# Softmax row sums of groups three to six by a VectorE reduction instead of ScalarE's accumulators

## The reference

```python
attn = jnp.einsum('bhtd,bhsd->bhts', q, k) * scale
attn = jnp.where(causal, -jnp.inf, attn)
attn = jax.nn.softmax(attn, axis=-1)
out = jnp.einsum('bhts,bhsd->bhtd', attn, v)
out = out.transpose(0, 2, 1, 3).reshape(b, t, NH * D)
return out @ Wo
```

## Time and profile before

| | |
|---|---|
| median of three runs | 156.2 us (156.09 to 156.68) |
| the profiled execution | 156.23 us |
| its span, first to last instruction | 154.4 us |
| granted TensorE clock, mean | 1.000 of full speed |
| TensorE matmuls busy | 148.3 us |
| VectorE busy | 118.5 us |
| ScalarE busy | 101.7 us |
| GpSimd busy | 60.0 us |

### The profile page before, as it was taken

One profiled execution on the slowest core, in us unless ns is written; L12 is line 12 of the kernel. 1 busy time (PEld: TensorE's weight loads), 2 busy tenths in 40 slices (PEclk: granted clock), 3 DMA queues, 4 the chain that ended last, 5 costly groups with the idle time before them and its releaser, 6 DMA issues.

```text
span 154.4 us, 3280 instructions
## 1 busy us (share of the span) xinstructions
PE 148.3 (96%) x1089; PEld 138.9 (90%) x1089; DVE 118.5 (77%) x370; ACT 101.7 (66%) x290; POOL 60.0 (39%) x50
## 2 busy tenths in 40 slices
PE   6999999999999999999999999799999999999992
PEld 2778789899998699999989999799999999999991
DVE  0058777898988967577765766999798995999792
ACT  0306997798999779998883496856456564654700
POOL 0004998454486344407326000334534336045100
PEclk9999999999999999999999999999999999999999
DMA  5999910000000299800000000000000000000004
GB/s 150 326 373 375 409 31 0 0 4 4 0 0 0 40 406 427 350 5 8 0 0 4 0 0 0 0 4 2 0 2 4 0 0 2 0 4 0 4 2 157
DMA packets 5891, 11.95 MB, mean 77 GB/s; under 512 B 930, under 2 KB 3698, under 8 KB 5746
## 3 DMA queue, kind: packets, MB, share of 16 engines
q1 hardware_dynamic: 4434, 9.79, 17.4%
q10 hardware_dynamic: 1440, 1.95, 3.6%
HBM read 11.13 MB, written 0.61 MB: 76 GB/s over the span
## 4 chain that ended last, share of the span: by engine, by line
PE 81%; DVE 7%; ACT 6%; DMA 3%; issue 1%; ACTq 1%; DVEq 0%
PE bank L1053 61%; PE bank L1142 5%; PE bank L1170 5%; PE bank L1077 3%; DMA x_sb<-xT 3%; PE bank L1068 2%; PE bank L1158 2%; ACT act L538 1%; ACT act_hi L541 1%; DVE hn L716 1%; ACT L545 1%; DVE stats L694 1%; PE bank L1097 1%; DVE h L839 1%; DVE rrest L809 0%
## 5 line engine op out<-in xcount | busy, mean ns | idle before, releaser
L411 POOL TENSOR_TENSOR exp_lo<-ffn_sb,exp_hi 128x512 fp32r<-128x512 f32 x18 | 24.2, 1351 | 43.4 <-ACT exp_hi L529 40.4
L842 DVE SCALAR_TENSOR_TENSOR h<-bank,gate,h 128x256 f32<-128x256 f32 (+1 forms) x80 | 32.7, 471 | 1.5 <-PE bank L1053 1.3
L1053 PE MATMUL bank<-exp_hi,act_hi 128*128 128x256 f32 (+1 forms) x90 | 25.7, 285 | 0.8 <-DVE h L842 0.8
L1053 PE MATMUL bank<-exp_hi,act_lo 128*128 128x256 f32 (+1 forms) x90 | 25.3, 281 | 0.0
L1053 PE MATMUL bank<-exp_lo,act_hi 128*128 128x256 f32 (+1 forms) x90 | 25.3, 281 | 0.0
L822 DVE TENSOR_TENSOR act_lo<-act,act_hi 128x256 fp32r<-128x256 f32 (+1 forms) x36 | 19.4, 571 | 3.4 <-ACT act_hi L541 3.0
L1053 PE MATMUL bank<-hnT_hi,exp_hi 128*128 128x256 f32 (+1 forms) x72 | 21.6, 300 | 0.0
L529 ACT ACTIVATE exp_hi<-ffn_sb 128x512 fp32r<-128x512 f32 x18 | 11.4, 635 | 15.3 <-PE bank L1053 15.3
L1053 PE MATMUL bank<-hnT_lo,exp_hi 128*128 128x256 f32 (+1 forms) x72 | 21.5, 298 | 0.0
L1053 PE MATMUL bank<-hnT_hi,exp_lo 128*128 128x256 f32 (+1 forms) x72 | 21.5, 298 | 0.0
L396 POOL TENSOR_TENSOR swapped<-swapped,sin_sb 128x512 f32<-128x512 f32 (+1 forms) x12 | 16.4, 1367 | 10.2 <-ACT swapped L496 10.1
(11 more groups left out here) (92 smaller groups left out, 370.7 us busy)
## 6 DMA issues: line engine op xcount, KB each, us to landing
ffn_sb<-w_ffn SPq DMA_DIRECT2D x6, 768.0 KB, 8.3
wqkv_sb<-w_qkv SPq DMA_DIRECT2D x4, 512.0 KB, 8.8
wo_sb<-w_o SPq DMA_DIRECT2D x1, 1024.0 KB, 11.1
x_sb<-xT ACTq DMA_DIRECT2D x2, 384.0 KB, 6.5
out<-h SPq DMA_DIRECT2D x2, 256.0 KB, 2.2
x_sb<-xT ACTq DMA_DIRECT2D x3, 128.0 KB, 4.6
wp_sb<-wpT SPq DMA_DIRECT2D x3, 128.0 KB, 3.7
wp_sb<-wpT ACTq DMA_DIRECT2D x3, 128.0 KB, 4.9
```

Source lines behind the costliest of these rows:

```text
L411: nc.gpsimd.tensor_tensor(exp_lo[:, e % SPLIT_RING, :], ffn_sb[:, e, :], exp_hi[:, e % SPLIT_RING, :].bitcast(F32), ALU.subtract).then_inc ...
L842: last = nc.vector.scalar_tensor_tensor(h[r, i, :], y, gate[r, i, one], h[r, i, :], ALU.mult, ALU.add)
L1053: last = nc.tensor.matmul(ps, a, b, start=(n == 0 and m == 0), stop=(n == len(pairs) - 1 and m == 2 and not more))
```

## The change

For groups 2 to 5, `exps` no longer adds up the rows. `inv_sum` begins with one VectorE `tensor_reduce` over the quad (111 x 4 rows of 111, or 74 x 4 rows of 74), which writes `ssum`, and waits on a new semaphore `sc_sum` before the reciprocal. Groups 0 and 1 stay as they were. With this, all four lists are written anew, from the first layer norm to the last expert; no step is added or dropped in them. The diff, with the stretches of the lists that matter most:

```diff
+SUMMED = 2
...
+        sc_sum = sem("sc_sum")
...
         @block.gpsimd
-            for n in range(0, 9):
+            for n in range(0, 8):
                 sine(n)
             normalise(0, 0)
+            sine(8)
             sine(9)
+            normalise(0, 1)
             sine(10)
-            normalise(0, 1)
             sine(11)
...
             normalise(2, 1)
+            low_parts(0)
             normalise(3, 0)
...
             def exps(g, c):
                 for j in range(QUAD):
                     hd = QUAD * c + j
                     scores_of = probs[0:GN[g], g % 2, hd, 0:GN[g]]
-                    last = nc.scalar.activation(scores_of, scores_of, ACT.Exp, bias=slow[0:GN[g], g, hd:hd + 1], scale=-1.0,
-                                                accum_out=ssum[0:GN[g], g, hd:hd + 1])
+                    less = slow[0:GN[g], g, hd:hd + 1]
+                    if g < SUMMED:
+                        last = nc.scalar.activation(scores_of, scores_of, ACT.Exp, bias=less, scale=-1.0,
+                                                    accum_out=ssum[0:GN[g], g, hd:hd + 1])
+                    else:
+                        last = nc.scalar.activation(scores_of, scores_of, ACT.Exp, bias=less, scale=-1.0)
                 last.then_inc(sc_exp, 1)
...
             def inv_sum(g, c):
                 dve.wait_ge(sc_exp, 2 * g + c + 1)
+                if g >= SUMMED:
+                    nc.vector.tensor_reduce(ssum[0:GN[g], g, QUAD * c:QUAD * c + QUAD], quad(probs, g, c),
+                                            AX_X, ALU.add).then_inc(sc_sum, 1)
+                    dve.wait_ge(sc_sum, 2 * (g - SUMMED) + c + 1)
                 nc.vector.reciprocal(sinv[0:GN[g], g, QUAD * c:QUAD * c + QUAD],
                                      ssum[0:GN[g], g, QUAD * c:QUAD * c + QUAD]).then_inc(sc_inv, 1)
```

More of the change, by code:

```diff
@@ L436, in _ @@
             normalise(5, 1)
-            for n in range(2, 18):
+            for n in range(1, 18):
                 low_parts(n)
@@ L593, in _ @@
             keep_pT(0, 1)
+            exps(1, 1)
             heads_high(0, 0)
@@ L878, in _ @@
             norm_apply(2)
+            norm_apply(3)
             turned_low(0)
             turned_low(1)
-            norm_apply(3)
             norm_stats(4)
@@ L886, in _ @@
             cosine(1)
+            turned_low(3)
             rope_add(0)
@@ L889, in _ @@
             cosine(3)
-            turned_low(3)
             turned_low(4)
-            rope_add(1)
-            rope_add(2)
+            for n in range(1, 4):
+                rope_add(n)
+            cosine(4)
+            cosine(5)
+            rope_add(4)
+            rope_add(5)
             wo_low()
-            cosine(4)
+            cosine(6)
             less_max(0, 0)
[L897 to L902, removed]
             cosine(7)
@@ L905, in _ @@
             rope_add(7)
+            inv_sum(0, 0)
+            less_max(0, 1)
+            less_max(1, 0)
             cosine(8)
-            less_max(1, 0)
             cosine(9)
+            inv_sum(0, 1)
             rope_add(8)
+            rope_add(9)
+            cosine(10)
+            rope_add(10)
             less_max(1, 1)
-            inv_sum(0, 1)
-            cosine(10)
             cosine(11)
-            for n in range(9, 12):
-                rope_add(n)
             inv_sum(1, 0)
+            rope_add(11)
+            less_max(2, 0)
             inv_sum(1, 1)
-            less_max(2, 0)
             heads_low(0, 0)
@@ L928, in _ @@
             less_max(4, 0)
+            less_max(4, 1)
+            heads_low(2, 0)
+            heads_low(2, 1)
             inv_sum(3, 0)
-            less_max(4, 1)
             inv_sum(3, 1)
@@ L977, in _ @@
             add_expert(1, 1)
-            act_low(6)
-            act_low(7)
             add_expert(1, 2)
+            for n in range(6, 9):
+                act_low(n)
             add_expert(2, 0)
@@ L983, in _ @@
             add_expert(2, 2)
-            act_low(8)
-            act_low(9)
             add_expert(3, 0)
             add_expert(3, 1)
-            act_low(10)
-            act_low(11)
+            for n in range(9, 13):
+                act_low(n)
             add_expert(3, 2)
@@ L998, in _ @@
             add_expert(5, 2)
+            for n in range(13, 16):
+                act_low(n)
             add_expert(6, 0)
-            for n in range(15, 18):
-                act_low(n)
             add_expert(6, 1)
             add_expert(6, 2)
+            act_low(16)
             add_expert(7, 0)
+            act_low(17)
             add_expert(7, 1)
@@ L1008, in _ @@
             add_expert(8, 1)
-            for n in range(18, 22):
+            act_low(18)
+            act_low(19)
+            add_expert(8, 2)
+            for n in range(20, 23):
                 act_low(n)
-            add_expert(8, 2)
             add_expert(9, 0)
@@ L1014, in _ @@
             add_expert(9, 2)
+            act_low(23)
             add_expert(10, 0)
-            for n in range(22, 27):
-                act_low(n)
             add_expert(10, 1)
@@ L1330, in _ @@
             down(1, 1)
-            up(8)
             down(1, 2)
             down(2, 0)
-            up(9)
+            for n in range(8, 12):
+                up(n)
             down(2, 1)
@@ L1355, in _ @@
             down(7, 0)
-            for n in range(17, 21):
-                up(n)
+            up(17)
+            up(18)
             down(7, 1)
@@ L1361, in _ @@
             down(8, 1)
+            up(19)
             down(8, 2)
-            up(21)
-            up(22)
+            for n in range(20, 24):
+                up(n)
             down(9, 0)
```

228 lines of the change are left out of this document (111 added, 117 removed).

## The result

The changed kernel takes 157.42 us (median of 5 runs, 157.07 to 157.71), the kernel before 156.6 in the same comparison. The ratio is 1.0056, 95% interval 1.0038 to 1.0074: 0.8 to 0.9 us slower, where I forecast 0.3 us faster, and outside my range (154.7 to 157.1). The profiled execution took 157.07 us with a span of 155.2, 0.8 more than before.

What follows compares the result with a forecast made beforehand. The prediction took TensorE to bound the kernel, busy 148.3 of 154.4 us. A walk through its waits took 0.3 us off the span, to 154.1; with the 1.83 us around it 155.9 us, range 154.7 to 157.1.

Steps and rivals of the forecast that it cites:

- Row sums cost nothing in the new lists: Groups 2 to 5: reductions add 4.2 us to VectorE, hidden between exps and normalise; at the high bound 0.8 us.
- Relief of ScalarE is not relief of the kernel: From 60 to 65 us ScalarE is busy for all 5.00 us, but so is TensorE; nobody waits for ScalarE.
- First layer norm, 0.1: norm_apply(3) ahead of turned_low(0) and (1) delays the first projection 0.55 us, but costs only 0.1 at cosine(0).
- First attention groups: From about 52 us: 0.6 and 0.3 us gained, given back by VectorE; TensorE through at 57.3 as before.
- Third output projection: It ends at 76.6, before 76.0, with turn_probs(4, ...) ahead of it and a short wait for heads_low(3, 1).
- Statistics, inv_std, two keep_pT, ..., 80.4: The fourth output projection waits for keep_turned(6) until 80.4, where before it was 80.57; gain 0.2 us.
- Router: router_exp ends at 94.4; the long TensorE stretch starts at 98.4, before 98.58: earlier 0.2 gain kept, nothing added.
- Experts, no wait: In the long TensorE stretch: the same 411-odd matmuls, and no wait found in the new order.
- The returned waits are not there: Faster rival: without the waits for heads_low(0, ...) and keep_turned(6), 1.2 us less, 154.7 us; chance 0.32.
- VectorE and GpSimd collide: Slower rival: rope_add(11) behind normalise(1, 0) delays scores(2, 1) by 1.0 us: 156.9, with slow sums 157.4; chance 0.14.
- A wait in the expert stage: Slower rival: six down pieces in a row outrun VectorE's sums, 0.5 to 1 us: 156.7 to 157; chance 0.09.
- Nothing moves: Rival: TensorE's work is the same and every gain is given back, 156.2 us; chance 0.12.

Runs made afterwards that it cites:

- the lists alone: New lists, with ScalarE's accumulators kept for all six groups and no reduction on VectorE, against the kernel before: 157.72 us, ratio 1.0080.
- the new tail alone: Old lists up to the last output projection, new lists from there on, accumulators kept, against the kernel before: 156.31 us, ratio 0.9979.

## Why the prediction was wrong

**What held.** The prices: 0.28 us a step for an exponential, reductions of 0.60 and 0.44, 3.0 us less on ScalarE (I took 2.9, of 2.9 to 5.4). *Row sums cost nothing in the new lists*: shown by the lists alone, which are not faster. *Relief of ScalarE is not relief of the kernel*: shown for the old lists without any sums (0.9996); in the new lists it is relief, of some 0.3 to 0.4 us. *First layer norm, 0.1*: 0.12 in the two profiles, but `project(2)` starts anywhere from 23.08 to 24.13 in the fourteen profiles, so this is not resolved.

**The step that failed** is the forecast that the returned waits between 52 and 81 us leave a gain of 0.2 us. They leave a loss of 0.9. By starts of equal work after `project(2)`, 0.2 to 0.3 us of it are there at `scores(3, 0)`, 0.4 come at `project_out(2)` and 0.35 behind `attend(4, 0)`; 0.1 is won back between them.

- *First attention groups, "net: nothing"*: +0.4 (0.26 after `project(2)`). I had VectorE's times right: `heads_low(0, 0)` and `(0, 1)` ended at 56.45 and 56.97, forecast 56.3 and 56.9. But I let TensorE be through 0.4 us after the second, and compared that with an end in the chain of before. By starts, `scores(3, 0)` begins at 57.56 after; where as much work was done before, `scores(3, 1)` less one score pair of 0.78, it was 57.18. The last releaser was also not only VectorE's list: `heads_high(0, 0)` stood behind `exps(1, 1)`, one of the quads that keep their accumulators.
- *Third output projection, "76.6"*: it ended at 77.36. Beside the 0.4 carried over, `project_out(2)` waited for `heads_low(3, 1)`. I called this "a short wait". The way from the last `attend` over `heads_high` and `heads_low` is 1.27 us (72.98 to 74.25), and only the transposes of group 4 and `scores(5, 1)`, 1.05 us, stand against it. The record shows 0.24 us of idle time; from start to start 0.40 are lost.
- *"Statistics, inv_std, two keep_pT, ..., 80.4"*: the sequence took 3.96 us, not 3.8, with `heads_low(4, ...)` (0.75) in front of `norm_apply(7)`, and both in front of `turned_low(6)`, which I had not on the path. My terms add up to 80.3, not 80.4. The rest of the error there, 81.32 for 80.4, is the late start. That this order costs the 0.35 us is shown: with tile 1's norm put back ahead of `attend(4, ...)` they are gone.
- *Router, "nothing added"*: too low by 0.36 in the other direction. The new tail does gain, which the run with the new tail alone shows.
- *Experts, no wait*: +0.14 (52.32 for 52.18); behind the old attention the same tail has only 0.04 of it (52.22), and the new lists with the accumulators have none (52.17), so the order alone does not make it. Not explained.

**The rivals.** *The returned waits are not there* was the opposite of what happened. *VectorE and GpSimd collide* did not come true: `rope_add(11)` took 0.86 us; GpSimd lost instead. Its times, 156.9 and 157.4 with slow sums, are the nearest to 157.42, by luck; the second does not follow either, since its terms give 157.7. *A wait in the expert stage*: 0.14 in place of 0.5 to 1. *Nothing moves* forecast 156.2 and was 0.8 to 0.9 us short. No rival of mine had what happened: a TensorE order with less work between an `attend` and the step that waits for its split, twice, and a norm's split listed behind work that it does not need. The signs that I named did come: `heads_lo` near 56 us and `hnT` in the chain (80.8 for 79), `router_exp` (95.3 for 94.4) and the long run (99.2 for 98.3) both 0.9 us late. They tell the places, not the gain.

## What to carry to other kernels

When lists of several engines are written anew, walk each dependence that leaves TensorE and returns (here 1.2 to 1.3 us over two engines) and count the TensorE work that stands against it in start times, not in drained ends: work that covered one such way is missing at another. A full engine is worth relieving only if something in the chain waits for it; a kernel with that work simply left out shows the ceiling at the price of one run, for the order of steps that it was run in. Test order and operation apart: here each half was slower than before, the two together no slower than either, and the one part that helped (the new tail) had nothing to do with the moved sums.

## What the hardware showed that I had not expected

An ACTIVATE with and without accumulator output has the same length, 380 ns for 111 columns (351 and 343 ns for 74); beyond that the output costs the read's step of 0.09 us. This is what the Trainium skill ("ScalarE: Activation LUTs", section on what ACT_TABLE_LOAD costs) leads to, and the trace now agrees.

GpSimd and VectorE, in the changed kernel, in order of time:

```profile
53.60 0.86 DVE L740 TENSOR_TENSOR qk<-qk,swapped 128x672 f32<-128x672 f32 x1
```

```profile
53.79 1.45 POOL L403 TENSOR_TENSOR probs<-probs,sinv 111x444 f32<-111x444 f32 x1 [0.74 <-DVE sinv L774]
```

The later of the two is held back: the product begins when the rotary sum has 0.67 us to go, and takes 1.45 us where it takes 0.93 alone. A reduction does not do this:

```profile
66.12 0.58 DVE L771 TENSOR_REDUCE ssum<-probs 111x4 f32<-111x444 f32 x1
```

```profile
66.34 1.81 POOL L403 TENSOR_TENSOR probs<-probs,sinv 111x444 f32<-111x444 f32 x2 [1.64 <-DVE sinv L774]
```

The row holds two products, the first of them begun inside the reduction. They take 1.81 us together, as in the kernel before, and the reduction 0.58 of its usual 0.60. The Trainium skill ("SBUF — State Buffer", section on who interferes with whom) has VectorE and GpSimd contend when VectorE reads two SBUF inputs, and never in a `tensor_reduce`; the traces agree with both.

VectorE's busy time rose by 1.1 us only, though the reductions are 4.2 us. By line, rotary sums fell from 13.0 to 11.4 us and the differences `act_lo` from 19.4 to 18.3, both operations with two SBUF inputs. The new order may have fewer of them beside GpSimd; this was not tested, and of the two forms of `act_lo` one fell (541 to 432 ns) and the other rose (602 to 649).
